# Moving the fp32 hidden activation of a feed-forward block from ScalarE to VectorE

## The reference

```
ff = relu(h @ ff_w1.T + ff_b1) @ ff_w2.T + ff_b2      # h: 256 x 256, hidden width 1024
return layernorm(h + ff, ln3_g, ln3_b)
```

## Time and profile before

| what | value |
|---|---|
| time, median of 3 runs | 845.6 us (844.19 to 856.61) |
| profiled execution, its own time | 844.19 us |
| its span | 842.3 us |
| mean granted TensorE clock | 0.967 |
| PE busy | 770.0 us (91%) |
| DVE busy | 632.2 us (75%) |
| ACT busy | 483.3 us (57%) |
| POOL busy | 486.8 us (58%) |
| first and last relu of line 1329 start at | 436.4 and 782.9 us |

### The profile page before, as it was taken

The page is one execution under the profiler, slowest core; times in us unless marked ns, Lnnn a source line. Parts: engine busy times, 40 slices in busy tenths (PEclk is TensorE's granted clock), DMA queues, the critical chain, the costliest instruction groups (busy, mean ns, idle before and its releaser), DMA issues.

```text
span 842.3 us, 19937 instructions
## 1 busy us (share of the span) xinstructions
PE 770.0 (91%) x7214; PEld 641.7 (76%) x7232; DVE 632.2 (75%) x1386; ACT 483.3 (57%) x1049; POOL 486.8 (58%) x598
## 2 busy tenths in 40 slices
PE   6898699999999898878799999999999998999886
PEld 4776578878887676555478888888888788899875
DVE  4444568787878988667989888987687767878774
ACT  5432265555665566556566666666666764666442
POOL 2323276777777676654346666666555785667542
PEclk9999999999999999899789999999999999999988
DMA  9584989688767764336432222222200020012222
GB/s 279 149 268 147 187 136 153 129 135 139 133 105 135 118 103 94 82 86 124 84 73 55 54 55 55 55 55 55 54 3 11 2 72 9 29 56 80 60 84 79
DMA packets 105308, 79.63 MB, mean 95 GB/s; under 512 B 43261, under 2 KB 101967, under 8 KB 104947
## 3 DMA queue, kind: packets, MB, share of 16 engines
q1 hardware_dynamic: 101850, 74.17, 42.1%
q10 hardware_dynamic: 3360, 4.18, 1.5%
HBM read 27.03 MB, written 12.97 MB: 47 GB/s over the span
## 4 chain that ended last, share of the span: by engine, by line
PE 66%; DVE 11%; issue 5%; SPq 3%; DMA 2%; ACT 2%; POOL 1%; POOLq 0%; DVEq 0%; ACTq 0%
PE a_misc L88 13%; PE a_pair L88 11%; PE a_s L1042 10%; PE a_pair L831 4%; PE a_pair L1003 4%; PE a_s L807 4%; PE a_pair L849 3%; PE a_pair L988 3%; PE a_s L805 3%; PE a_s L965 2%; PE a_s L88 2%; PE a_pair L1141 2%; DVE c_z L1558 1%; PE a_pair L852 1%; DVE a_nm L1456 1%
## 5 line engine op out<-in xcount | busy, mean ns | idle before, releaser
L1456 DVE TENSOR_REDUCE a_nm<-a_s 128x2 f32<-128x512 f32 (+1 forms) x192 | 127.1, 678 | 50.8 <-PE a_s L807 50.1
L1208 ACT ACTIVATE a_pT<-a_pair 128x512 f32<-128x512 f32 x192 | 113.6, 597 | 82.0 <-PE a_pair L831 74.3
L1958 POOL TENSOR_TENSOR c_hidden<-c_hid,c_hidden 128x256 fp32r<-128x256 f32 x128 | 95.5, 747 | 80.0 <-ACT c_hidden L1337 76.6
L1303 ACT ACTIVATE a_pT<-a_pair 77x512 f32<-77x512 f32 x128 | 76.0, 594 | 103.2 <-PE a_pair L988 100.6
L1042 PE MATMUL a_s<-c_w,c_hidden 128*128 128x256 f32 x768 | 118.8, 294 | 2.0 <-POOL c_hidden L1958 2.0
L1865 POOL TENSOR_SCALAR_AFFINE_SELECT a_pT<-a_pT 128x256 f32<-128x256 f32 (+1 forms) x192 | 92.4, 500 | 27.3 <-ACT a_pT L1208 26.7
L1042 PEld LDWEIGHTS a_s<-c_w,c_hidden 128*128 128x128 f32 x768 | 100.1, 192 | 2.8 <-POOL c_hidden L1958 2.4
L88 PE MATMUL a_pair<-c_fxh,c_w 128*128 128x256 f32 x512 | 99.9, 287 | 0.0
L831 PE MATMUL a_pair<-a_sq,a_sk 98*128 98x256 bf16 (+1 forms) x512 | 76.0, 252 | 8.5 <-ACT a_pT L1208 7.3
L1620 DVE TENSOR_REDUCE a_nm<-a_s 128x5 f32<-128x385 f32 (+1 forms) x96 | 54.7, 569 | 37.8 <-PE a_s L965 37.4
L807 PE MATMUL a_s<-a_sk,a_sq 96*128 96x256 bf16 (+1 forms) x512 | 74.5, 247 | 8.5 <-DMA a_sk<-a_parts 4.2
(11 more groups left out here) (273 smaller groups left out, 2163.1 us busy)
## 6 DMA issues: line engine op xcount, KB each, us to landing
a_sq<-a_parts SPq DMA_DIRECT2D x96, 128.0 KB, 4.4
a_sk<-a_parts SPq DMA_DIRECT2D x96, 128.0 KB, 4.6
a_sq<-c_parts SPq DMA_DIRECT2D x96, 128.0 KB
x<-in_xT SPq DMA_DIRECT2D x16, 256.0 KB, 6.5
res<-in_x SPq DMA_DIRECT2D x16, 256.0 KB, 5.7
out<-g_fin SPq DMA_DIRECT2D x16, 256.0 KB, 2.1
a_sk<-kc_parts SPq DMA_DIRECT2D x96, 38.5 KB
fold_rows<-x_fold ACTq DMA_DIRECT2D x1, 2496.0 KB, 9.6
```

What stands on the lines that cost most here:

```text
L1208: nc.scalar.activation(pT[g % NPT][:], stps[g % 2][:], ACT.Exp).then_inc(s_exp, 1)
L1303: nc.scalar.activation(pT[g % NPX][0:SC], st_ps[0:SC, :], ACT.Exp).then_inc(c_exp, 1)
L1456: nc.vector.tensor_reduce(nm[c % 2][:, QT * heads[0] + qt:QT * heads[-1] + qt + 1:QT], sps[g % 2][:].rearrange("p (h k) -> p h k", h=len(h ...
L1958: nc.gpsimd.tensor_tensor(hl(m), hid[n % NHID][:], f32(hh(m)), ALU.subtract).then_inc(c_hl, 1)
```

## The change

ACT's two instructions for a hidden tile become one: relu with bias straight from PSUM into the rounded high part. The fp32 value, which only POOL still needs, is now made by DVE from the same PSUM buffer with one instruction (add the bias, then maximum with 0). DVE waits for `c_hh`, so it comes after ACT's read of the buffer, and POOL waits for DVE's `c_hid` where it waited for ACT's `c_hh`. `up_tile` on PE still waits for `c_hid`, which is now set by DVE. ACT's instruction stands where the first of the two stood, right behind the slot's exponentials.

```
-            def hidden(n):                                   # ACT
-                act.wait_ge(c_up, n + 1)
-                atleast(act, c_hl, n - NHID + 1)
-                nc.scalar.activation(hid[n % NHID][:], up[n % 2][:, 0:S], ACT.Relu, bias=b1[:, m:m + 1]).then_inc(c_hid, 1)
             def hidden_high(n):                              # ACT
-                act.wait_ge(c_hid, n + 1)
+                act.wait_ge(c_up, n + 1)
                 atleast(act, c_down, n - FT + 1)
-                nc.scalar.activation(hh(m), hid[n % NHID][:], ACT.Copy).then_inc(c_hh, 1)
+                nc.scalar.activation(hh(m), up[n % 2][:, 0:S], ACT.Relu, bias=b1[:, m:m + 1]).then_inc(c_hh, 1)
 ACT, cross_slot:
                 cross_exps(g - CST_LAG)
-                hidden(g - UP_LAG - 1)
+                hidden_high(g - UP_LAG - 1)
...
-                hidden_high(g - UP_LAG - 1)
+            def hidden(n):                                   # DVE
+                dve.wait_ge(c_hh, n + 1)
+                atleast(dve, c_hl, n - NHID + 1)
+                nc.vector.tensor_scalar(hid[n % NHID][:], up[n % 2][:, 0:S], b1[:, m:m + 1], 0.0, ALU.add, ALU.max).then_inc(c_hid, 1)
 DVE, cross_slot:
                     deviation(n - 3, s - 6)
+                hidden(g - UP_LAG - 1)
                 if s == 0:
                     cross_turn_av(n - 2, 0)
 POOL, hidden_low:
-                pool.wait_ge(c_hh, n + 1)
+                pool.wait_ge(c_hid, n + 1)
```

More of the change, by code:

```diff
@@ L1321, in weight_high, with hidden_high @@
                 nc.scalar.activation(hi, src, ACT.Copy).then_inc(c_wh, 1)
-            def hidden(n):
+            def hidden_high(n):
                 c, m = divmod(n, FT)
@@ L1327, in hidden @@
                 act.wait_ge(c_up, n + 1)
-                atleast(act, c_hl, n - NHID + 1)
-                nc.scalar.activation(hid[n % NHID][:], up[n % 2][:, 0:S], ACT.Relu, bias=b1[:, m:m + 1]).then_inc(c_hid, 1)
-            def hidden_high(n):
-                c, m = divmod(n, FT)
-                if not real(c):
-                    return
-                act.wait_ge(c_hid, n + 1)
                 atleast(act, c_down, n - FT + 1)
-                nc.scalar.activation(hh(m), hid[n % NHID][:], ACT.Copy).then_inc(c_hh, 1)
+                nc.scalar.activation(hh(m), up[n % 2][:, 0:S], ACT.Relu, bias=b1[:, m:m + 1]).then_inc(c_hh, 1)
             def cross_slot(n, s):
@@ L1688, in cross_moments @@
                 nc.vector.bn_aggr(t.mv[:, n, :], stat2[:]).then_inc(c_agg, 1)
+            def hidden(n):
+                c, m = divmod(n, FT)
+                if not real(c):
+                    return
+                dve.wait_ge(c_hh, n + 1)
+                atleast(dve, c_hl, n - NHID + 1)
+                nc.vector.tensor_scalar(hid[n % NHID][:], up[n % 2][:, 0:S], b1[:, m:m + 1], 0.0, ALU.add, ALU.max).then_inc(c_hid, 1)
             def feed_residual(c):
```

## The result

The change made the kernel slower, by less than 1%: 856.9 us as the median of 20 runs (849.3 to 860.0) against 851.6 us of the kernel before (20 runs, 844.2 to 856.6). The ratio is 1.0065, with a 95% interval of 1.0044 to 1.0087, which is 5.5 us. The prediction had 2.5 us over the profiled execution of before.

The account below looks back on a forecast made before the run. PE was taken as the bound, with DVE second. Terms 0 + 0 + 2 + 1 + 1.5 - 2 = +2.5 us on 844.2 gave 846.7, rounded to 847 us; forecast 842 to 855 us (0.67), wider range 838 to 860.

Parts of the forecast that it names:

- ACT's relief, 0: Removing ACT's copies, 52.9 us of busy time, buys 0 because nothing on PE's path waits for ACT; 1 us gain as end.
- The new instruction, 425 ns: DVE's added instruction takes 425 ns, as a PSUM-to-SBUF copy does, 54.4 us in all; a 478 ns row bounds it above.
- Quiet blocks, 0: Cross-stage blocks where PE has no gap: DVE rises to 20.1 of 21.0 us and still fits, costing 0.
- The walk through slot 0: Timeline check of a quiet block: DVE's added work there leaves PE's slot 1 up tile 0.2 us to spare.
- First block, +2: At 441 to 462 us DVE would need 23.1 of 21 us, costing 2 us (ends +1 and +3).
- group-chain block, +1: At 525 to 546 us a four-element chain brings DVE to 21.3 us; 1 us for this block and the next.
- The port, -2: Near 694 us POOL's low part must wait for DVE's centrings, so PE's 4.01 us gap shortens by about 2 us.
- 600 to 783 us, +1.5: Late stretch: DVE isn't full, but its steps queue behind relu waits; 1.5 us in all (ends 0 and +6).
- The chains have about a slot of slack.: After 600 us, DVE's gated-stage work behind the new instruction could be delayed by about a slot without holding PE.
- up to 0.7 us: After 600 us, a relu in the same slot comes at most this much later than DVE could take it.
- DVE sets the pace: Slower rival: PE's up tiles wait for DVE in slots 1 and 7 of every block; 866 us, chance 0.15.
- POOL's new pace frees DVE: Faster rival: POOL, held back by its new wait, stops delaying DVE everywhere, so PE's waits go; 840 us, chance 0.16.

Follow-up runs that it names:

- the load put back: The changed kernel with an unread 128x256 copy added on ACT at the end of each slot, where the removed copy stood; 856.2 us, ratio 1.0069.
- the run with a constant: The changed kernel with constant 0 replacing the bias column in DVE's new instruction, the bias left out of the fp32 value; 854.2 us, ratio 1.0061.
- the last run: The changed kernel with ACT's relu first, DVE's new instruction ahead of every chain, and POOL waiting in slot 0 for the centrings; 855.5 us, ratio 1.0116.
- the first split: Batch elements 0 to 6 as in the changed kernel, 7 to 15 on ACT as before, POOL waiting in slot 1; 851.1 us, ratio 1.0021.

## Why the prediction came out as it did

**ACT's relief, 0.** Right, as far as the load put back can tell. The gaps of PE from 436 to 800 us, which the prediction gives as some 13 us, are 14.3 (364 us less 349.7 busy); this changes nothing in the argument.

**The new instruction, 425 ns.** Wrong by 54: 479. The bound from above was the better neighbour, because it shares the per-partition operand, which the run with a constant prices at 59 ns. The experiment also shows that the time hung on it little.

**Quiet blocks, 0.** Right: 21.03 us in both, and PE stays full. The walk through slot 0 had 0.2 us to spare, and the shorter centring gave 0.3 more. DVE has 18.93 us there and not 20 or more, since POOL holds it up less.

**First block, +2, and group-chain block, +1.** Of the right sign: +0.93, just under the lower end of 1, and +1.45. DVE had 20.29 us in the first block; the sum said 2.1 us over, and less than half of that came. The group chain cost at 546 to 567 us and not in the block before, whose row the prediction used.

**The port, -2.** The mechanism was right and shown by two experiments that add nothing but a wait on POOL. The gap of 4.01 us behind the slow centring is gone. The row was read short, though: not only the second centring was passed. The first alone took 2.08 us, until 696.02 us, and POOL's lines 1994 and 1958 both ended before that, at 695.02 and 695.70. But the prediction took it at one place and as a net gain. In that stretch another wait appeared at once, 2.83 us at 706.47, because the deviation chain in slot 0 is open to POOL just as the centring was.

**600 to 783 us, +1.5.** This is the step that failed: "The chains have about a slot of slack." The walk through slots 0 and 1 was made for a quiet block alone and carried over. In a quiet block PE has the twelve matmuls of the query projection there, 1.44 us. In the late blocks they have ended (in the rows around 706 us PE has only the two transposes of line 1111 and the six matmuls of line 1042 between its slot 0 tile and the wait), so PE comes to slot 1's up tile sooner, while on DVE the chain of slot 0 is stretched by POOL's steps. After 600 us PE waits for the new instruction 11.6 us in 10 times, where the prediction had at most some 8 delays, at its end of +6. Six blocks there cost 7.45 us in the traces, or 2.3 at full clock, where I had +1.5 and -2 together, and the run with the change in the late elements alone has a ratio of 1.0070, as large a loss as the whole. The "up to 0.7 us" by which a relu would be late had no row behind it, either: DVE waits for the relu 28.6 us in 28 times, up to 3.0 us. What stays open is how such a wait turns into time. Moving the instruction of slot 0 ahead of its chain ended the waits in slot 1 but took little off at full clock (131.0 to 130.5 us), and the last run ended all of them and is 1.2% slower than before. Lateness behind a chain is one form that the cost takes; the work itself costs in another place when it is moved.

**The rivals.** The signature of "DVE sets the pace", an up tile that waits for `c_hid` in slots 1 and 7, is in the trace 11 times (5 and 6), but in no quiet block; the rival's 866 us needed every block. The first half of its mechanism is what happened, in fewer blocks. "POOL's new pace frees DVE" is real and amounts to 0.8 to 1.0% when it comes alone. The two are both in the change and work against each other: POOL's pace is worth 5 us of product in slot 1 and 7 in slot 0, the work on DVE costs 9 to 14 with POOL held back in both kernels, and 8 are left in the change as it was made.

**Still open.** Where the 5 us of the first split lie that its blocks don't show, and with them how the loss divides between early and late elements. By which path the last run loses its 14 us, of which the waits shown give 7 or so. And how much of the loss would go with more PSUM buffers for the up tile, which wasn't tried: it is the plain rival to all the moves above, as PE waits only because the buffer is not free.

## What to carry to other kernels

An engine that isn't the bound can take more work without loss only in those stretches where each thing that waits for it has slack; walk every kind of block, above all those in which the bounding engine has lost part of its work, since there it comes to its next wait sooner. When a change moves work and also a wait, try the wait alone: here it was the whole gain. And before an instruction is moved forward in its queue, look at when its input arrives: here, early in the queue and late in its input (1.0203 and 1.0267) was worse than late in both (1.0065). Last, one trace per kernel carries the chance of its clock: take that out before two traces are compared, and look whether the runs bear out what is left.

## What the hardware showed that I had not expected

A VectorE `tensor_scalar` of 128x256 from PSUM takes 420 ns with two constants and 479 ns with one per-partition operand.

Steps of DVE on 2 elements per partition, 0.15 to 0.17 us at their best, took up to 1.24 us beside a POOL instruction in the rows above, and one wait on POOL that keeps the two apart made the whole kernel 1.0% faster (839.7 us). The Trainium skill (SBUF — State Buffer, on the shared port pair) says that the loser is blocked for the whole instruction of the other; the rows at 702.38 and 703.65 us agree, each step ends with the POOL instruction beside it. The first centring of the earlier trace rows was held over two POOL instructions, which is more than that.

Two waits of PE in the late stretch, of 1.98 and 2.83 us, were followed by a granted clock at the 1.2 GHz level (0.50 over 684.3 to 687.7 us and 708.2 to 715.0 us); one of 1.97 us in the kernel before was not.
